# An RWKV block in fp32 on one core: five hand-written orders of steps are replaced by five others

## The reference, cut to what matters

```python
xn = _ln(x, ln1_w, ln1_b)
sx = _token_shift(xn, state[:, i1])
xxx = jnp.tanh((xn + sx * maa_x) @ maa_w1).reshape(b, l, 5, 1, EXTRA_MAA)
xxx = jnp.matmul(xxx, maa_w2).reshape(b, l, 5, E)
x5 = xn[:, :, None] + sx[:, :, None] * (maa_stack + xxx)
w = jnp.exp(-jnp.exp(time_decay + jnp.tanh(x5[:, :, 1] @ decay_w1) @ decay_w2))
r, k, v = x5[:, :, 3] @ Wr.T, x5[:, :, 0] @ Wk.T, x5[:, :, 2] @ Wv.T   # by heads
g = jax.nn.silu(x5[:, :, 4] @ Wg.T)
def step(s, rkvw):
    r_t, k_t, v_t, w_t = rkvw
    a = k_t[:, :, :, None] * v_t[:, :, None, :]
    out = jnp.einsum('bhk,bhkd->bhd', r_t, u * a + s)
    return (a + w_t[:, :, :, None] * s, out)
...
att = group_norm(outs) * gn_w + gn_b
x = x + att * g @ Wo.T
xn2 = _ln(x, ln2_w, ln2_b); sx2 = _token_shift(xn2, state[:, i0])
rr = jax.nn.sigmoid((xn2 + sx2 * ffn_maa_r) @ ffn_Wr.T)
kk = jnp.square(jax.nn.relu((xn2 + sx2 * ffn_maa_k) @ ffn_Wk.T))
x = x + rr * (kk @ ffn_Wv.T)
```

## Time and profile before

| | |
|---|---|
| three executions | 508.1, 508.7, 509.38 us |
| the profiled execution | 509.58 us |
| its span, first to last instruction | 507.8 us |
| PE busy | 473.6 us, 93% |
| DVE busy | 473.3 us, 93% |
| ACT busy | 282.1 us, 56% |
| POOL busy | 85.6 us, 17% |
| mean granted TensorE clock | 1.000 |
| chain that ended last | DVE 40%, PE 16%, issue 13% of the span |

### The profile page before, as it was taken

One profiled execution on the slowest core, in us unless ns is written; L12 is line 12 of the kernel. 1 busy time (PEld: TensorE's weight loads), 2 busy tenths in 40 slices (PEclk: granted clock), 3 DMA queues, 4 the chain that ended last, 5 costly groups with the idle time before them and its releaser, 6 DMA issues.

```text
span 507.8 us, 6207 instructions
## 1 busy us (share of the span) xinstructions
PE 473.6 (93%) x2172; PEld 275.6 (54%) x2172; DVE 473.3 (93%) x528; ACT 282.1 (56%) x612; POOL 85.6 (17%) x93
## 2 busy tenths in 40 slices
...
DMA packets 26999, 69.49 MB, mean 137 GB/s; under 512 B 1624, under 2 KB 19928, under 8 KB 24536
## 3 DMA queue, kind: packets, MB, share of 16 engines
...
## 4 chain that ended last, share of the span: by engine, by line
DVE 40%; PE 16%; issue 13%; POOL 1%; ACT 1%; DVEq 0%; POOLq 0%
DVE kv L624 16%; DVE kv L632 6%; DVE x L530 5%; DVE kv L614 4%; PE pa L952 3%; PE pc L959 3%; PE pc L952 2%; DVE att L642 1%; DVE sq L679 1%; POOL kv L445 1%; PE patt L1124 1%; DVE xr L683 1%; DVE bonus L590 1%; DVE th L583 1%; PE pc L1164 1%
## 5 line engine op out<-in xcount | busy, mean ns | idle before, releaser
L624 DVE TENSOR_TENSOR_SCAN kv<-w_sb,kv 128x512 f32<-128x512 f32 (+2 forms) x144 | 146.8, 1084 | 0.1
L952 PE MATMUL pa<-x,large_sb 128*128 128x512 f32 (+2 forms) x272 | 113.6, 560 | 4.5 <-DVE x L539 3.3
L952 PEld LDWEIGHTS pa<-x,large_sb 128*128 128x128 f32 x272 | 50.0, 190 | 60.6 <-issue 47.4
L632 DVE TENSOR_TENSOR kv<-kv,r_sb 128x2048 f32<-128x2048 f32 (+2 forms) x36 | 73.3, 2045 | 0.2
L614 DVE TENSOR_TENSOR kv<-vrep,k_sb 128x2016 f32<-128x2016 f32 (+2 forms) x34 | 70.1, 2063 | 0.0
L445 POOL COPY kv<-s_sb 128x32 f32<-128x32 f32 (+2 forms) x36 | 33.7, 941 | 133.9 <-PE patt L1124 125.7
L414 POOL DMA_DIRECT2D x<-xn x21 | 19.7, 937 | 172.1 <-DVE x L530 172.1
L530 DVE SCALAR_TENSOR_TENSOR x<-pb,vec_sb,sx 128x512 f32<-128x512 f32 (+1 forms) x64 | 42.7, 708 | 0.2 <-PE pb L1030 0.2
L1124 PE MATMUL patt<-kv,const_sb 128*32 128x512 f32 (+2 forms) x288 | 34.5, 556 | 2.6 <-DVE kv L632 2.4
L996 PE MATMUL pb<-th,w_sb 32*128 32x512 f32 (+2 forms) x100 | 34.2, 606 | 1.5 <-DVE x L530 1.5
L755 ACT ACTIVATE xres<-pc 128x256 f32<-128x256 f32 x29 | 10.7, 384 | 40.4 <-PE pc L1164 40.4
...
## 6 DMA issues: line engine op xcount, KB each, us to landing
vrep<-v_scratch SPq DMA_DIRECT2D x12, 2048.0 KB, 15.9
x<-xn POOLq DMA_DIRECT2D x18, 512.0 KB, 7.8
...
x_tok<-in_x SPq DMA_DIRECT2D x6, 512.0 KB, 11.5
...
xres<-in_x SPq DMA_DIRECT2D x6, 512.0 KB, 11.2
out<-xres SPq DMA_DIRECT2D x6, 512.0 KB, 8.1
out<-trr POOLq DMA_DIRECT2D x6, 512.0 KB, 6.0
```

Of the source, the lines that this page charges most:

```text
L624: ins = dve.tensor_tensor_scan(flat, w_sb[:, p, q % HF, 0:nb].rearrange("p b t -> p (b t)"), flat, 0.0, ALU.mult, ALU.add)
L632: dve.tensor_tensor(flat, flat, r_sb[:, p, q % HF:q % HF + 1, 0:n].broadcast_to([P, G4, n]), ALU.mult).then_inc(rs_ready, 1)
L952: ins = pe.matmul(dst[:, m, 0:n], w(a)[:, m * P:(m + 1) * P], src[:, a, :], start=(a == 0), stop=(a == HF - 1))
```

## The change

All five step lists are replaced. No step is added or dropped, `WARM` stays as it was, and every step does what it did. The buffer `bn` is declared as `max(SUBS, extent(0)[2])` rows, which is 3 as before. The heads of two lists and a line of the third:

```diff
 DVE_STEPS = """
-    st1.0 nrm1.0 shift.0 cwv.0 mix0.0 mix3.0 mix2.0 mix1.0 cs0.0 a0.0 a1.0 rk.0 shift.1 mix4.0 sc0.0 bonus.0
+    st1.0 nrm1.0 shift.0 cwv.0 cs0.0 mix0.0 mix3.0 mix2.0 mix1.0 a0.0 a1.0 rk.0 mix4.0 shift.1 sc0.0 sc1.0 rs0.0
...
 PE_STEPS = """
-    T1.0 W1.0 X01.0 X2.0 X3.0 P0.0 D1.0 VS.0 D2.0 P1.0 P3.0 T1.1 X4.0 CB.0 P4.0 W1.1 X01.1 BO.0 S0.0 P0.1 X2.1
+    T1.0 W1.0 X01.0 X2.0 X3.0 P0.0 D1.0 P1.0 D2.0 VS.0 T1.1 P3.0 X4.0 P4.0 W1.1 CB.0 X01.1 BO.0 S0.0 P0.1 X2.1
...
 SP_STEPS = """
-    lx.0 vst.0 lx.1 lx.2 vl1.0 vl0.0 lr.0 lx.3 vst.1 vl0.1 lx.4 vl1.1 vst.2 sx2.0 vl0.2 lr.1 lx.5 vl1.2 vst.3
+    lx.0 lx.1 lx.2 vst.0 vl0.0 vl1.0 vst.1 vl0.1 lx.3 lr.0 vl1.1 vst.2 vl0.2 sx2.0 lr.1 lx.4 lx.5 vl1.2 vst.3
...
-        bn = sb("bn", [P, SUBS, 8])
+        bn = sb("bn", [P, max(SUBS, extent(0)[2]), 8])
```

More of the change, by code:

```diff
@@ L47 @@
-    out.5 a0.7 shift.8 a1.7 bonus.7 gate.6 sc0.7 rs0.7 mix0.8 mix1.8 a2.7 mix2.8 sc1.7 mix3.8 rs1.7 shift2.6
-    sc2.7 a3.7 mix4.8 rs2.7 sc3.7 rs3.7 out.6 rk.8 a0.8 bonus.8 a1.8 gate.7 sc0.8 rs0.8 sc1.8 a2.8 rs1.8 sc2.8
+    st1.0 nrm1.0 shift.0 cwv.0 cs0.0 mix0.0 mix3.0 mix2.0 mix1.0 a0.0 a1.0 rk.0 mix4.0 shift.1 sc0.0 sc1.0 rs0.0
+    bonus.0 mix0.1 a2.0 mix1.1 sc2.0 mix2.1 rs1.0 mix3.1 a3.0 rs2.0 mix4.1 sc3.0 rs3.0 rk.1 bonus.1 shift.2 a0.1
+    gate.0 sc0.1 mix0.2 mix1.2 rs0.1 a1.1 mix2.2 sc1.1 mix3.2 shift2.0 a2.1 rs1.1 sc2.1 a3.1 mix4.2 sc3.1 rs2.1
@@ new lines @@
+    rs3.1 rk.2 out.0 shift.3 a0.2 bonus.2 sc0.2 gate.1 rs0.2 mix0.3 mix1.3 a1.2 mix2.3 sc1.2 mix3.3 rs1.2 a2.2
+    shift2.1 mix4.3 a3.2 sc2.2 sc3.2 rs2.2 rs3.2 rk.3 out.1 a0.3 shift.4 bonus.3 sc0.3 gate.2 mix0.4 mix1.4 a1.3
+    rs0.3 mix2.4 sc1.3 mix3.4 rs1.3 shift2.2 mix4.4 a2.3 a3.3 sc2.3 sc3.3 rs2.3 rs3.3 rk.4 out.2 shift.5 a0.4
+    bonus.4 sc0.4 gate.3 mix0.5 a1.4 mix1.5 rs0.4 sc1.4 mix2.5 rs1.4 mix3.5 a2.4 shift2.3 mix4.5 a3.4 sc2.4
+    sc3.4 rs2.4 rs3.4 rk.5 out.3 a0.5 bonus.5 shift.6 sc0.5 gate.4 mix0.6 mix1.6 a1.5 rs0.5 mix2.6 sc1.5 a2.5
@@ L49 @@
+    mix3.6 shift2.4 mix4.6 rs1.5 sc2.5 a3.5 rs2.5 sc3.5 rs3.5 rk.6 out.4 a0.6 shift.7 bonus.6 sc0.6 gate.5
+    mix0.7 mix1.7 a1.6 rs0.6 sc1.6 mix2.7 a2.6 mix3.7 rs1.6 shift2.5 sc2.6 a3.6 rs2.6 mix4.7 sc3.6 rk.7 rs3.6
+    out.5 a0.7 a1.7 shift.8 bonus.7 gate.6 sc0.7 rs0.7 mix0.8 mix1.8 a2.7 mix2.8 sc1.7 mix3.8 rs1.7 shift2.6
+    mix4.8 a3.7 sc2.7 sc3.7 rs2.7 rs3.7 rk.8 out.6 a0.8 a1.8 bonus.8 gate.7 sc0.8 rs0.8 sc1.8 a2.8 rs1.8 sc2.8
     a3.8 shift2.7 rs2.8 sc3.8 rs3.8 gate.8 out.7 gate.9 gate.10 st2.8 st2.9 nrm2.8 st2.10 nrm2.9 shift2.8
```

52 lines of the change are left out of this document (26 added, 26 removed).

## The result

| | before | after |
|---|---|---|
| median of the executions | 508.71 us (508.1 to 509.38) | 513.83 us (512.56 to 518.8, four) |
| the profiled execution | 509.58 us, span 507.8 | 514.6 us, span 512.8 |
| mean granted clock | 1.000 | 0.993 |

The ratio is 1.0107 (95%: 1.007 to 1.0143): slower by 5.1 us. The forecast was 510.2, with a range up to 513.3. The sign was right, the size was not.

The account below looks back on a forecast made before the run. VectorE, hardly ever waiting between 75 and 437 us, was taken as the bound. Its idle-time terms, +1.9 - 0.4 + 1.1 - 1.1 = +1.5 us, gave 511.1 us from the profiled execution, 510.2 from the median; range 506.8 to 513.3.

Parts of the forecast that it names:

- the path that `P0.0` and `D1.0` take is in the same chain and needs no term of its own: Step for chunk 0's opening: this TensorE path adds nothing beyond the opening's +1.9 us.
- VectorE is busy from there to the end of its last read, so this reaches the end: Last-chunk step: the 1.1 us won at `gate.7` carries through to the kernel's end.
- The opening, +1.9: Chunk 0: centring before the mixes returns as a wait ahead of `a0.0`; first scan at 36.3, costing 1.9 us.
- Chunk 1, -0.4: `S3.0` no longer delays `CB.1`, so the 2.22 us bonus wait shrinks; gain 0.4 us, between 0 and 0.7.
- Chunk 4, +1.1: `lx.7` ahead of `vl0.4` on SyncE delays that load, so `a0.4` waits; cost 1.1 us, between 0 and 2.9.
- The last chunk, -1.1: `a1.8` fills the 1.86 us wait ahead of `bonus.8`, so `gate.7` starts earlier; gain 1.1 us, between 0.5 and 1.6.
- Everything else, 0: Some 140 steps per list between 75 and 437 us, moved by one or two places; 0, bounds 0 and +3 us.
- The clock drop: Rival: longer wait ahead of `P0.0` brings TensorE's 1.2 GHz level, projections slow; +2 to +4 us, 513 us; chance 0.05.
- The late load: Rival: `vl1.2`, behind a store and residual on SyncE, lands late for `a1.2`; 0 to 3 us more, 513; chance 0.18.

Follow-up runs that it names:

- e_best1: Kernel before with VectorE's new last-chunk order (`e_last_dve`), plus `rk.1` moved behind `rs3.0` in chunk 1; 507.98 us, ratio 0.9963.
- e_lx7_bo8: `e_bo8` with one SyncE step back: the x load `lx.7` again behind `vl1.4`; 522.22 us, ratio 1.024 to the kernel before.
- e_last_dve: Kernel before with only VectorE's new last-chunk order (`rk.8` ahead of `out.6`, `bonus.8` behind `a1.8`); 508.24 us, ratio 0.9971.
- e_fill: Changed kernel plus eleven filler matmuls on TensorE in chunk 0, in front of `X2.0`, `P4.0` and `BO.0`; 515.66 us, ratio 1.0122 to the kernel before.
- e_fill_bo8: `e_fill` with TensorE's `BO.8` put back behind `WO.7`; 511.69 us, ratio 1.0049 to the kernel before.
- e_bo8: Changed kernel with one TensorE step put back, `BO.8` behind `WO.7`; 512.69 us, ratio 1.0061 to the kernel before.

## Why the prediction was wrong

The profiled execution took 514.6 us where the sum gave 511.1. **Two steps of the prediction failed.** The first is the sentence that "the path that `P0.0` and `D1.0` take is in the same chain and needs no term of its own": half clock there and at 45 us cost some 1.9 us. The second is "VectorE is busy from there to the end of its last read, so this reaches the end": 1.0 us came back in the tail. The rest, some 0.6 us, is made up of the small terms below. Point by point, in its order:

- **The opening, +1.9.** Right as a sum of orders: the first scan without the half clock is at 36.52, forecast 36.3, by way of a centring from 15.4 and a wait of 4.15 us ahead of `a0.0`. A part of that match is luck, since such starts scatter by 0.8 us; the 17.38 us from the first mix on, forecast 17.35, are the better sign. The waits at `rk.0` and `mix4.0`, 0.61 and 0.41 us, came where one of about 1.3 us at `mix4.0` was forecast. Wrong was that `P0.0` and `D1.0` need no term: at half clock `P0.0` took 1.66 us longer, and the first scan came 18.49 instead of 17.38 us behind the first mix, 1.1 us. The first mix itself came 1.18 us late, forecast 0.77, since the state's load went out at 8.55 instead of 7.97. The whole delay was 3.40 us.
- **Chunk 1, -0.4.** 2.22 became 1.65, against it 0.32 at `mix4.1`: the net is -0.25. But in `e_best1` the move of `rk.1` alone gave 0.2 of the 0.6 that I put down to `S3.0`; so the rest of it comes from other steps around, which ones I didn't test.
- **Chunk 4, +1.1.** It was 0.57, within the bounds. `nrm.5` ended at 211.96, not 209.2, and the landing took 13.84 us. The sign of `lx.7`'s place, however, was misread: `e_lx7_bo8` shows that in the new order it saves some 9 us.
- **The last chunk, -1.1.** Up to `gate.7` so (0.29 + 0.42 left of 1.86), and `e_last_dve` has the gain to the end. What failed is "so this reaches the end". I counted VectorE's new order and not `BO.8` ahead of `WO.7` beside it on TensorE. The work that it puts off, the output projection of chunk 7 with its norm and `T2.7`, stands in front of `S1.8`, and the wait came back at `a3.8`: 0.90 us in the profiled execution. By the times with and without the swap it is 2.3 us, but 1.0 of the profiled pair's 2.1 us arose ahead of it.
- **Everything else, 0.** 0.45 at `shift2.0`, 0.20 and 0.19 at `mix3.1` and `sc2.3`, and 0.81 at `a2.0` that went with the second half clock (neither it nor the wait is in `e_fill`). Against what I wrote, the tails' order isn't quite the same in both: ScalarE and GpSimd have a step or two swapped there. It cost nothing: the kernel is 4.99 us late at `a3.8` and 5.0 at the end.
- **The rivals.** The clock drop had 0.05 and came, at the place named, for 1.1 us at the first scan and 0.8 at `a2.0` where 2 to 4 were priced. What I held against it, a clock of 1.000 in the one profile, was too little: of 29 executions of the kernel before on the chip of the tail's runs, 13 have a clock of 0.992 or 0.993 and take 510.5 us, against 509.3 of the 16 at 1.0. The Trainium skill's rule (TensorE: Matmul & The Clock Gate, What's actually happening), that the array is at half by default and activity releases it, pointed the right way. The late load came as far as its issue (113.10 instead of 98.47), and its reader didn't wait.

Put together by the profiled executions' spans, 507.8 us before, 509.3 with both accidents out (`e_fill_bo8`), 510.7 with the half clock back (`e_bo8`) and 512.8 in the changed kernel: the orders' own waits cost 1.5 us, just what the sum forecast (in part by terms that cancel: chunk 4 cost 0.5 us less, the small waits 0.6 more), and the accidents 3.5. By the ratios the same steps are 0.49%, 0.12% and 0.46%, each give or take 0.2 to 0.4%, so the shares aren't sure, and by the medians on their own chip the orders cost 2.1 us. The shares shift because half clock and the tail depend on when things meet: `e_bo8` lost 0.6 us to half clock at 130 us, where the changed kernel lost nothing, the changed kernel 0.9 us at 45, and what the opening gives can make the tail's power fall into a bad place, as in `e_fill`.
